# Two-layer graph attention on one core: the attention product of layer 1 computed graph by graph, with the high and low halves of h stacked over the rows

## The chip, the cores and the metric

The kernel runs on one core of a Trainium2 chip. Its engines work side by side and are tied by semaphores: TensorE (PE; its weight loads are shown apart, as PEld), VectorE (DVE), ScalarE (ACT), GpSimd (POOL), and SyncE (SP), which here only starts DMAs. The metric is the device time of one execution in microseconds (us). Less is better.

## The reference, cut to what matters

128 graphs of 64 nodes with 768 features pass through two layers, each with layer norm, relu, attention within the graph, and a residual. Layer 0 has 6 heads of 128 and the usual query, key, value and output projections. Layer 1 has 12 heads of 64:

```python
h = maximum(layernorm(x), 0)                     # 768 features of a node
hh = einsum('bnd,ade->bane', h, W)               # 12 heads of 64: "h" of the kernel
th = tanh(hh)
attn = th @ w_src + swapaxes(th @ w_dst, 2, 3)   # one number per pair of nodes and head
attn = softmax(where(adj, leaky(attn, 0.2), -999))
o = elu(einsum('banm,bame->bane', attn, hh) + b) # the product that is changed
gate = sigmoid(h @ H_w.T + H_b)
x = x + gate * o + (1 - gate) * h
```

## The kernel before, in words

Two graphs of 64 nodes fill the 128 partitions: that is a tile. Two tiles (t = 0, 1) make a group, and there are 32 groups. The program runs as a pipeline over groups. In step i the engines do layer 0 of group i, most of layer 1 of group j = i - 1, and the attention product and output of layer 1 of group p = i - 2. Steps 0, 1 and the last three are written out; the others are one loop body. Nothing is scheduled by a program: each engine has its own list of work, in the order in which `one(i, ...)` stands in its block, and waits on semaphores.

All large products use fp16 with a high and a low half for each operand. A product a*b is made of three fp16 matmuls, hi*hi + hi*lo + lo*hi, which add up in PSUM.

The order of PE in a step of the loop is: queries of i (two halves, L582), with the attention product of p for tile 0 behind them (`attend1`, L592 to L599); keys of i, with the attention product for tile 1 between their halves; values of i, tile 0; scores of layer 0 (L673, fp32); values, tile 1; the projection of j with W (`project_h`, tiles 0 and 1, L570); the gate's projection of tile 0; the context of layer 0 (L684); the operands of the logits of layer 1 (`logit_operands`, L702 and L706); the gate's projection of tile 1; the logits (L719); the output projection of layer 0. Each projection of one tile is 36 matmuls. `logit_operands` waits for `g_ready` of tile 0, since it writes into the PSUM bank that the gate's projection of tile 0 has filled and that DVE's `gate_argument` (L1100) reads.

What stands between the projection with W and that wait: ACT takes tanh (L1473) and the fp16 high half of h (L1477) out of PSUM. DVE takes the low half (`h_low`, L1082). POOL multiplies tanh by w_src and w_dst (`products`, L1690, L1691), and DVE sums over each head (L1072, L1077), splits the sums in three bf16 parts (L1110 to L1116) and then does `gate_argument` (L1100). POOL's products of tile 1 wait for `dst_ready` of tile 0, because both tiles use the same scratch. On DVE the order is: low part of h, source and target sums of tile 0; source sum, low part of h, target sum of tile 1; split; gate argument of tile 0.

The attention product of layer 1 works on a whole tile. The probabilities P of one head and tile are 128 x 64 (rows are the nodes of both graphs). They are written as fp16 high (ACT, `p1_high`, L1408) and low (DVE, `p1_low`, L926) halves into `e1`, where blocks of 64 columns alternate with zeroed gaps (POOL, L1737). SP's DMA transposes (L478) read graph 0 and graph 1 at offsets that differ by one block. So each head arrives in `pt1` as a 128 x 128 matrix with the two graphs on its diagonal and zeros elsewhere. It is the stationary operand of three matmuls of 64 columns per head; 12 heads make 36 matmuls per tile.

Of the kernel before, what the change touches and what calls it, by code (L numbers as in the profile page):

```python
# [25 lines left out]
F16 = mybir.dt.float16  # L26
# [3 lines left out]
ALU = mybir.AluOpType  # L30
# [51 lines left out]
def build_two_layer_gnn(nc, x, adj, wq, bq, wk, bk, wv, bv, wf, bf, wl, b1, w_src, w_dst, wg, bg, out):  # L82
# [13 lines left out]
    with ExitStack() as ctx:  # L96
# [72 lines left out]
        def split(first, shape, **k):  # L169

            v = units(first, 2).bitcast(F16)
            return [v[:, n * 2 * C:(n + 1) * 2 * C].rearrange(shape, **k) for n in range(2)]

        h1v_hi, h1v_lo = split(0, "p (t c) -> p t c", t=T)
        gate = tiles(2)
# [31 lines left out]
        e0 = spread(19 * C)  # L207
        e1 = spread(past_qt)

# [18 lines left out]
        spent = [w[:, WQ:WF + 1].rearrange("p m k n -> p (m k n)").bitcast(F32) for w in (w_hi, w_lo)]  # L228
        end_flat = w_lo[:, WQ].rearrange("p k n -> p (k n)")[:, 0:2 * SPREAD]
        end_e1 = [end_flat[:, n * SPREAD:(n + 1) * SPREAD] for n in range(2)]  # L230
        end_pt1 = halves(arena, 17 * C, a=H1)
# [204 lines left out]
        def _(sp):  # L436
# [32 lines left out]
            def transpose_rows(n, part, ht, g):  # L469
                after_held(sp, transposes_held, (hi_made, lo_made)[part][n], 2 * g + 2 if n else 2 * g)  # L470
                for t in range(T):
                    sp.dma_start_transpose(ht[:, :, t * P:(t + 1) * P], (h_hi, h_lo)[part][:, t, :])\  # L472
                        .then_inc(ht_landed[n], DMA)

            def transpose_blocks(pt, e, landed):
                for g in range(2):
                    r = slice(N * g, N * g + N)
                    sp.dma_start_transpose(pt[:, :, r], e[r, (1 - g) * N:(1 - g) * N + 2 * C]).then_inc(landed, DMA)  # L478

            def one(i, now, mid, last, nxt):  # L480
# [4 lines left out]
                def first_probabilities(g, zeroed):  # L485
                    after_held(sp, transposes_held, p1_gaps, zeroed)
                    after_held(sp, transposes_held, p1_hi_made, 2 * g + 1)
                    transpose_blocks(pt1[0][0], e1[0], pt1_hi_landed[0])
                    after_held(sp, transposes_held, p1_lo_made, 2 * g + 1)
                    transpose_blocks(pt1[0][1], e1[1], pt1_lo_landed[0])  # L490

                def second_probabilities():
                    sp.wait_ge(p1_hi_made, 2 * p + 2)
                    transpose_blocks(end_pt1[0], end_e1[0], pt1_hi_landed[1])
                    sp.wait_ge(p1_lo_made, 2 * p + 2)
                    transpose_blocks(end_pt1[1], end_e1[1], pt1_lo_landed[1])

# [16 lines left out]
                if last:  # L514
                    after_held(sp, transposes_held, p1_hi_made, 2 * p + 2)
                    after_held(sp, transposes_held, sum1_ready, 2 * p + 1)
                    transpose_blocks(pt1[1][0], e1[0], pt1_hi_landed[1])
                if mid:
# [5 lines left out]
                if last:  # L524
                    after_held(sp, transposes_held, p1_lo_made, 2 * p + 2)
                    after_held(sp, transposes_held, sum1_ready, 2 * p + 2)
                    transpose_blocks(pt1[1][1], e1[1], pt1_lo_landed[1])
                if mid:
# [32 lines left out]
        def _(pe):  # L561
# [30 lines left out]
            def attend1(t, g):  # L592
                for a in range(H1):
                    c = slice(a * E1, (a + 1) * E1)
                    pt1_hi, pt1_lo = pt1_of(t, g)
                    parts = ((pt1_hi, h1v_hi), (pt1_hi, h1v_lo), (pt1_lo, h1v_hi))
                    for n, (pt, hv) in enumerate(parts):
                        mm = nc.tensor.matmul(pair_att[t][:, c], pt[:, a, :], hv[:, t, c], start=(n == 0), stop=(n == 2))  # L598
                mm.then_inc(o_psum, 1)  # L599
# [25 lines left out]
            def one(i, now, mid, last, nxt):  # L625
# [30 lines left out]
                def attend(t):  # L656
                    if t == 0:
                        pe.wait_ge(h_ready, 2 * p + 2)
# [147 lines left out]
        def _(dve):  # L806
# [121 lines left out]

# [86 lines left out]
            def one(i, now, mid, last, nxt):  # L1015
                j, p = i - 1, i - 2
                first = isinstance(i, int) and i == 0
                tail, final = mid and not now, last and not mid
                def h_low(t):
                    dve.wait_ge(th_ready, 2 * j + t + 1)  # L1020
# [59 lines left out]
                def h_low(t):  # L1080
                    dve.wait_ge(h_hi_ready, 2 * j + t + 1)
                    nc.vector.scalar_tensor_tensor(h1v_lo[:, t, :], pair_prj[t][:, 0:C], HV, h1v_hi[:, t, :],  # L1082
                                                   ALU.mult, ALU.subtract).then_inc(h_ready, 1)

# [290 lines left out]
        def _(act):  # L1375
# [22 lines left out]
            def p1_high(t, g):  # L1398
# [57 lines left out]
            def one(i, now, mid, last, nxt):  # L1456
# [8 lines left out]
                def h_parts(t):  # L1465
# [145 lines left out]
        def _(pool):  # L1611
# [36 lines left out]
            def one(i, now, mid, last, nxt):  # L1648
# [82 lines left out]
                if mid:  # L1731
                    keep_copy()
                    products(0)
                    products(1)
                    target_terms()
                    after_held(pool, gaps_held, ct_psum, 2 * i + 2)
                    nc.gpsimd.memset(gaps(past_qt), 0.0).then_inc(p1_gaps, 1)  # L1737
                    if not nxt:
                        nc.gpsimd.memset(gaps_in(end_flat), 0.0).then_inc(end_gaps, 1)
                if now:  # L1740
# [38 lines left out]
```

## Time and profile before

| | |
|---|---|
| time, median of 3 runs | 2560.9 us (2559.81 to 2561.69) |
| time of the profiled execution | 2561.74 us |
| its span | 2559.9 us |
| PE busy | 2498.9 us, 98% of the span |
| DVE busy | 2003.8 us, 78% |
| ACT, POOL busy | 908.3 us (35%), 804.6 us (31%) |
| one step of the loop | 77.2 us |
| granted TensorE clock, mean | 0.99 of full speed |

The profiled execution lies 1.84 us above its own span, and within 1 us of the median. The page lists busy time by engine and by group of instructions. The timeline view lists instructions with their start, and so shows who is late at a given place. In it, lengths of matmuls include their way through the array; the rate of a row of matmuls is read from starts. PE's row of instructions in one step repeats every 77.2 us almost to the hundredth, so one step stands for all of them.

### The profile page before, as it was taken

How to read it: one execution, taken by the hardware profiler on the slowest of the kernel's cores; microseconds unless marked ns; L12 is line 12 of the kernel's file. 1: busy time of each engine (PE TensorE's matmuls, PEld its weight loads, DVE VectorE, ACT ScalarE, POOL GpSimd, SP SyncE). 2: the span in 40 equal slices, each digit the busy share in tenths (PEclk: the TensorE clock that was granted, in tenths of full speed). 3: DMA queues.
4: the chain of work that ended last, by engine and by line, in shares of the span. 5: the costliest groups of instructions: out<-in, count | busy, mean ns of one | idle time of the engine just before them, and what ended most of it. 6: DMA issues, size and time to landing. Idle time of an engine off the chain costs nothing.

```text
span 2559.9 us, 51824 instructions
## 1 busy us (share of the span) xinstructions
PE 2498.9 (98%) x21440; PEld 1789.9 (70%) x21440; DVE 2003.8 (78%) x2704; ACT 908.3 (35%) x1054; POOL 804.6 (31%) x564
## 2 busy tenths in 40 slices
PE   7999999999999999999999999999999999999995
PEld 5766777776777776777766777766777766777763
DVE  7768777778787788777787787787787787787778
ACT  5333333233333333333333333333333343332332
POOL 1133332333332333322333323333323333323334
PEclk9999999999999999999999999999999999999997
DMA  8243343443343443443433443433433433434432
GB/s 297 44 76 80 80 99 74 80 81 76 83 96 73 84 80 74 86 92 69 92 75 75 90 87 74 91 72 77 93 83 75 89 73 76 97 79 75 81 58 54
DMA packets 552301, 216.94 MB, mean 85 GB/s; under 512 B 517840, under 2 KB 527056, under 8 KB 552272
## 3 DMA queue, kind: packets, MB, share of 16 engines
q1 hardware_dynamic: 552272, 216.53, 40.6%
q8 instruction: 21, 0.34, 0.1%
q14 instruction: 8, 0.07, 0.0%
HBM read 67.02 MB, written 25.17 MB: 36 GB/s over the span
## 4 chain that ended last, share of the span: by engine, by line
PE 94%; DVE 3%; ACT 1%; DMA 1%; POOL 0%; SPq 0%; issue 0%; DVEq 0%
PE pair_prj L570 56%; PE pair_prj L582 29%; PE pair_att L684 3%; PE pair_att L598 3%; PE pair_att L673 2%; PE pair_att L719 1%; DMA arena<-in_L_gnn_Wq 0%; DVE w_lo L865 0%; PE pair_prj L706 0%; PE pair_prj L608 0%; SPq L472 0%; DVE w_top L825 0%; SPq L478 0%; POOL arena L1660 0%; DVE w_hi L954 0%
## 5 line engine op out<-in xcount | busy, mean ns | idle before, releaser
L570 PE MATMUL pair_prj<-w_hi,arena 128*128 128x512 f16 (+1 forms) x6144 | 1443.7, 327 | 6.4 <-DVE arena L1082 6.1
L570 PE MATMUL pair_prj<-w_lo,arena 128*128 128x512 f16 (+1 forms) x3072 | 1003.2, 327 | 0.0
L570 PEld LDWEIGHTS pair_prj<-w_hi,arena 128*128 128x128 f16 x6144 | 601.8, 98 | 416.0 <-issue 10.4
L582 PE MATMUL pair_prj<-arena,w_hi 128*128 128x256 f16 x4608 | 762.3, 273 | 3.5 <-DVE w_lo L872 3.3
L582 PE MATMUL pair_prj<-arena,w_lo 128*128 128x256 f16 x2304 | 629.3, 273 | 0.0
L582 PEld LDWEIGHTS pair_prj<-arena,w_hi 128*128 128x128 f16 x4608 | 447.4, 98 | 55.6 <-issue 3.4
L570 PEld LDWEIGHTS pair_prj<-w_lo,arena 128*128 128x128 f16 x3072 | 301.2, 98 | 199.5 <-issue 2.5
L1638 POOL TENSOR_TENSOR rstd<-var_eps,minus_half 128x2 f32<-128x2 f32 x63 | 62.8, 997 | 695.4 <-DVE var_eps L890 688.5
L582 PEld LDWEIGHTS pair_prj<-arena,w_lo 128*128 128x128 f16 x2304 | 225.9, 98 | 26.6
L1655 POOL TENSOR_TENSOR arena<-arena,b_row 128x768 f32<-128x768 f32 x60 | 108.6, 1809 | 331.0 <-DVE arena L947 331.0
L1388 ACT ACTIVATE h_hi<-arena,shift,rstd 128x768 f16<-128x768 f32 x124 | 120.6, 1020 | 215.0 <-DVE shift L895 215.0
L1690 POOL TENSOR_TENSOR arena<-arena,src_row 128x768 f32<-128x768 f32 x62 | 113.6, 1832 | 246.0 <-ACT arena L1473 246.0
L1660 POOL TENSOR_TENSOR arena<-arena 128x768 f32<-128x768 f32 x60 | 126.5, 2108 | 152.5 <-ACT arena L1419 152.5
L907 DVE TENSOR_TENSOR arena<-arena,h_hi 128x768 f16<-128x768 f32 x124 | 161.4, 1342 | 3.6 <-ACT arena L1388 3.6
L1424 ACT ACTIVATE arena<-arena 128x768 f32<-128x768 f32 x60 | 50.7, 845 | 283.1 <-DVE arena L954 283.1
L911 DVE SCALAR_TENSOR_TENSOR arena<-pair_prj,w_undo,bk_col 128x768 f32<-128x768 f32 x64 | 65.1, 1018 | 109.6 <-PE pair_prj L582 109.6
L1691 POOL TENSOR_TENSOR arena<-arena,dst_row 128x768 f32<-128x768 f32 x62 | 132.8, 2142 | 0.0
L1419 ACT ACTIVATE arena<-arena,keep_shift,keep_rstd 128x768 f32<-128x768 f32 x60 | 61.2, 1020 | 192.0 <-DVE arena L975 192.0
L1388 ACT ACTIVATE arena<-arena,shift,rstd 128x768 f32<-128x768 f32 x128 | 123.7, 1013 | 11.6 <-DVE shift L895 6.2
L877 DVE BATCH_NORM_STATS2 bn_out<-arena 128x6 f32<-128x384 f32 x252 | 121.7, 545 | 2.3 <-DMA arena<-in_x 2.3
L1745 POOL TENSOR_TENSOR arena<-arena,bf_row 128x768 f32<-128x768 f32 x64 | 115.6, 1828 | 6.1 <-DVE bf_row L1149 6.1
L1487 ACT ACTIVATE arena<-arena 128x768 f32<-128x768 f32 x62 | 52.4, 844 | 183.1 <-DVE arena L1100 183.1
(180 smaller groups left out, 2905.6 us busy)
## 6 DMA issues: line engine op xcount, KB each, us to landing
arena<-in_x SPq DMA_DIRECT2D x64, 768.0 KB, 4.3
out<-arena SPq DMA_DIRECT2D x64, 384.0 KB, 2.3
arena<-arena SPq DMA_TRANSPOSE x380, 3.4
arena<-in_L_gnn_Wq SPq DMA_DIRECT2D x2, 1152.0 KB, 8.5
arena<-in_L_gnn_Wk SPq DMA_DIRECT2D x2, 1152.0 KB, 11.8
w_hi<-in_L_gnn_Wv SPq DMA_DIRECT2D x2, 1152.0 KB, 13.5
w_lo<-in_L_gnn_Wf SPq DMA_DIRECT2D x2, 1152.0 KB, 14.4
arena<-in_L_gnn_W SPq DMA_DIRECT2D x2, 1152.0 KB, 13.2
```

Source lines behind the costliest of these rows:

```text
L570: mm = nc.tensor.matmul(pair[:, lo:hi], lhs(a, k), weight(m, k, b)[:, lo:hi], start=(k == 0 and n == 0), stop=(k == KT - 1 and n == 2))
L582: mm = nc.tensor.matmul(pair[:, c * 256:(c + 1) * 256], weight(m, k, a)[:, o:o + P], (ht0_hi, ht0_lo)[b][:, k, :], start=(k == 0 and n == ...
L598: mm = nc.tensor.matmul(pair_att[t][:, c], pt[:, a, :], hv[:, t, c], start=(n == 0), stop=(n == 2))
L684: mm = nc.tensor.matmul(pair_att[t][:, h * P:(h + 1) * P], v[:, t, h * P:(h + 1) * P], pt[:, t * H0 + h, :], start=(n == 0), stop=(n == 2))
L877: bn = nc.vector.bn_stats(bn_out[n][:, t, c, :], src[:, t, c * (C // 2):(c + 1) * (C // 2)])
L907: nc.vector.tensor_tensor(h_lo[:, t, :], rows[:, t, :], h_hi[:, t, :], ALU.subtract)\
L1388: return nc.scalar.activation(dst[:, t, :], src[:, t, :], ACT.Relu, bias=shift[n][:, t:t + 1], scale=rstd[n][:, t:t + 1])
L1655: nc.gpsimd.tensor_tensor(o, o, b1_row[:].unsqueeze(1).broadcast_to([P, H1, E1]), ALU.add)\
L1660: nc.gpsimd.tensor_tensor(held(g)[:, t, :], held(g)[:, t, :], scratch(t, g)[2], ALU.add)\
L1690: nc.gpsimd.tensor_tensor(by_src, th, src_row[:], ALU.mult).then_inc(src_prod, 1)
L1691: nc.gpsimd.tensor_tensor(by_dst, th, dst_row[:], ALU.mult).then_inc(dst_prod, 1)
L1745: nc.gpsimd.tensor_tensor(x1[:, t, :], x1[:, t, :], bf_row[:], ALU.add).then_inc(bf_added, 1)
```

## The change

The product P*h of layer 1 is computed for each graph of a tile apart. For graph b, the high half of h (64 nodes) is placed on partitions 0 to 63 and the low half on partitions 64 to 127 of one operand, `h1v[b]`. The probabilities are transposed so that P_hi of a head stands on both halves of the partitions. One matmul over 128 rows then gives P_hi*h_hi + P_hi*h_lo. A second one, with P_lo above and zeros below, adds P_lo*h_hi. The stationary operand is 64 columns wide, and graph b writes PSUM partitions 64b to 64b + 63.

- PE: per head 2 x 2 matmuls with a 64-column stationary operand, in place of 3 with 128 columns; 48 per tile in place of 36.
- ACT: `p1_high` writes each block of 64 twice (1536 elements per partition in place of 768). The high half of h is taken graph by graph, in two instructions over 64 partitions.
- DVE: `h_low` becomes two instructions over 64 partitions. One reads PSUM and the high half and writes 64 partitions further up. `p1_low` keeps its size.
- POOL: only the gaps of the low halves are zeroed, 768 elements in place of 1664.
- SP: the transposes of probabilities read 128 partitions x 768 each, in place of 64 x 1536; their number stays. The counts of `h_ready` and `h_hi_ready` double.

```diff
-        h1v_hi, h1v_lo = split(0, "p (t c) -> p t c", t=T)
+        h1v = split(0, "p (t c) -> p t c", t=T)
...
+            def transpose_heads(pt, e, landed):
+                for n in range(2):
+                    a = slice(n * H0, (n + 1) * H0)
+                    sp.dma_start_transpose(pt[:, a, :], e[:, a].rearrange("p a z n -> p (a z n)")).then_inc(landed, DMA)
...
-                    parts = ((pt1_hi, h1v_hi), (pt1_hi, h1v_lo), (pt1_lo, h1v_hi))
-                    for n, (pt, hv) in enumerate(parts):
-                        mm = nc.tensor.matmul(pair_att[t][:, c], pt[:, a, :], hv[:, t, c], start=(n == 0), stop=(n == 2))
+                    for n, pt in enumerate((pt1_hi, pt1_lo)):
+                        for b in range(2):
+                            r = slice(b * N, (b + 1) * N)
+                            mm = nc.tensor.matmul(pair_att[t][r, c], pt[:, a, r], h1v[b][:, t, c],
+                                                  start=(n == 0), stop=(n == 1))
...
-                    pe.wait_ge(h_ready, 2 * j + t + 1)
+                    pe.wait_ge(h_ready, 4 * j + 2 * t + 2)
...
-                nc.vector.scalar_tensor_tensor(blocks(e_lo), p1[:, t], P_TOP, blocks(e_hi), ALU.mult, ALU.subtract)\
-                    .then_inc(p1_lo_made, 1)
+                nc.vector.scalar_tensor_tensor(e_lo[:, :, 0, :], p1[:, t], P_TOP, e_hi[:, :, 0, :], ALU.mult,
+                                               ALU.subtract).then_inc(p1_lo_made, 1)
...
-                    dve.wait_ge(h_hi_ready, 2 * j + t + 1)
-                    nc.vector.scalar_tensor_tensor(h1v_lo[:, t, :], pair_prj[t][:, 0:C], HV, h1v_hi[:, t, :],
-                                                   ALU.mult, ALU.subtract).then_inc(h_ready, 1)
+                    for b in range(2):
+                        dve.wait_ge(h_hi_ready, 4 * j + 2 * t + b + 1)
+                        nc.vector.scalar_tensor_tensor(h1v[b][N:P, t, :], pair_prj[t][b * N:(b + 1) * N, 0:C], HV,
+                                                       h1v[b][0:N, t, :], ALU.mult, ALU.subtract).then_inc(h_ready, 1)
...
-                nc.scalar.activation(blocks(e1_of(t, g)[0]), p1[:, t], ACT.Copy, scale=P_TOP).then_inc(p1_hi_made, 1)
+                nc.scalar.activation(e1_of(t, g)[0], p1[:, t].unsqueeze(2).broadcast_to([P, H1, 2, N]), ACT.Copy,
+                                     scale=P_TOP).then_inc(p1_hi_made, 1)
...
-                    nc.scalar.activation(h1v_hi[:, t, :], pair_prj[t][:, 0:C], ACT.Copy, scale=HV)\
-                        .then_inc(h_hi_ready, 1)
+                    for b in range(2):
+                        nc.scalar.activation(h1v[b][0:N, t, :], pair_prj[t][b * N:(b + 1) * N, 0:C], ACT.Copy, scale=HV)\
+                            .then_inc(h_hi_ready, 1)
...
-                    nc.gpsimd.memset(gaps(past_qt), 0.0).then_inc(p1_gaps, 1)
+                    nc.gpsimd.memset(e1[1][:, :, 1, :], 0.0).then_inc(p1_gaps, 1)
```

PE in the loop, from the last query matmul to the first key matmul, tile 0 (L582 is the projection, L598 the attention product), before:

```order
L582 MATMUL pair_prj1<-arena,w_hi 128x256 x2
L582 MATMUL pair_prj1<-arena,w_lo 128x256
L598 MATMUL pair_att0<-arena 128x64 [waits pt1_lo_landed0,pt1_hi_landed0,h_ready]
L598 MATMUL pair_att0<-arena 128x64 x35
L582 MATMUL pair_prj0<-arena,w_hi 128x256 [waits q_ready]
```

And in the changed kernel (L588 and L605 are the same two lines):

```order
L588 MATMUL pair_prj1<-arena,w_hi 128x256 x2
L588 MATMUL pair_prj1<-arena,w_lo 128x256
L605 MATMUL pair_att0<-arena 64x64 [waits pt1_lo_landed0,pt1_hi_landed0,h_ready]
L605 MATMUL pair_att0<-arena 64x64 x47
L588 MATMUL pair_prj0<-arena,w_hi 128x256 [waits q_ready]
```

The 36 matmuls have become 48, with moving operand and neighbours in the same order; only their shape and number differ.

DVE in the loop, from the low parts of the next group's layer 0 to the split of the sums (L1082 is `h_low`, L1072 and L1077 the source and target sums), before:

```order
L1082 SCALAR_TENSOR_TENSOR arena<-pair_prj0,arena 128x768 [waits h_hi_ready]
L1072 TENSOR_REDUCE src_dst<-arena 128x12 [waits src_prod]
L1077 TENSOR_REDUCE src_dst<-arena 128x12 [waits dst_prod]
L1072 TENSOR_REDUCE src_dst<-arena 128x12 [waits src_prod]
L1082 SCALAR_TENSOR_TENSOR arena<-pair_prj1,arena 128x768 [waits h_hi_ready]
L1077 TENSOR_REDUCE src_dst<-arena 128x12 [waits dst_prod]
L1110 CAST parts<-src_dst 128x4x12 [waits dst_ready,src_ready]
```

And in the changed kernel (L1086 is `h_low`, L1075 and L1080 the sums; ISA and REGISTER_ALU compute the values of waits):

```order
L1086 SCALAR_TENSOR_TENSOR arena<-pair_prj0,arena 64x768 [waits h_hi_ready]
L1085 REGISTER_ALU
L1086 SCALAR_TENSOR_TENSOR arena<-pair_prj0,arena 64x768 [waits h_hi_ready]
L1075 TENSOR_REDUCE src_dst<-arena 128x12 [waits src_prod]
L1080 TENSOR_REDUCE src_dst<-arena 128x12 [waits dst_prod]
L1075 TENSOR_REDUCE src_dst<-arena 128x12 [waits src_prod]
L1085 REGISTER_ALU
L1086 SCALAR_TENSOR_TENSOR arena<-pair_prj1,arena 64x768 [waits h_hi_ready]
L1085 REGISTER_ALU
L1086 SCALAR_TENSOR_TENSOR arena<-pair_prj1,arena 64x768 [waits h_hi_ready]
L1080 TENSOR_REDUCE src_dst<-arena 128x12 [waits dst_prod]
L1114 CAST parts<-src_dst 128x4x12 [waits dst_ready,src_ready]
```

Each `h_low` has become two instructions; the second pair stands between the source and the target sum of tile 1.

## Rows read from the trace of the kernel before

**Rows 1.** Page, busy time, share of the span and instructions.
```profile
PE 2498.9 (98%) x21440; PEld 1789.9 (70%) x21440; DVE 2003.8 (78%) x2704; ACT 908.3 (35%) x1054; POOL 804.6 (31%) x564
```

**Rows 2.** Windows view of one steady group: span, then busy time (count) by engine.
```profile
1002.10:1079.30 77.20, 77.20 (x671) 55.46 (x669) 60.77 (x82) 27.11 (x33) 24.95 (x17) 1.00 0.41 82
```

**Rows 3.** Timeline, weight loads, in the steady group and in the tail: start, length, what.
```profile
1079.25 0.18 PEld L702 LDWEIGHTS pair_prj<-node_eye,dst_terms 128*108 128x108 bf16 x2
...
2519.71 0.17 PEld L702 LDWEIGHTS pair_prj<-node_eye,dst_terms 128*108 128x108 bf16 x2 [3.85 <-POOL dst_terms L1697]
```

**Rows 4.** Timeline, DVE, from the first low part of h.
```profile
1069.37 0.94 DVE L1082 SCALAR_TENSOR_TENSOR arena<-pair_prj,arena 128x768 f16<-128x768 f32 x1
1070.24 0.94 DVE L1072 TENSOR_REDUCE src_dst<-arena 128x12 f32<-128x768 f32 x1
1071.15 0.95 DVE L1077 TENSOR_REDUCE src_dst<-arena 128x12 f32<-128x768 f32 x1
1074.46 0.95 DVE L1072 TENSOR_REDUCE src_dst<-arena 128x12 f32<-128x768 f32 x1 [2.36 <-POOL arena L1690]
1075.33 0.95 DVE L1082 SCALAR_TENSOR_TENSOR arena<-pair_prj,arena 128x768 f16<-128x768 f32 x1
1076.22 0.95 DVE L1077 TENSOR_REDUCE src_dst<-arena 128x12 f32<-128x768 f32 x1
...
1078.10 1.01 DVE L1100 SCALAR_TENSOR_TENSOR arena<-pair_prj,w_undo,bg_row 128x768 f32<-128x768 f32 x1
```

**Rows 5.** Timeline, POOL then ACT, the same stretch.
```profile
1072.62 1.81 POOL L1690 TENSOR_TENSOR arena<-arena,src_row 128x768 f32<-128x768 f32 x1 [1.50 <-ACT arena L1473]
...
1071.64 0.90 ACT L1473 ACTIVATE arena<-pair_prj,w_undo 128x768 f32<-128x768 f32 x1 [4.25 <-PE pair_prj L570]
1072.44 0.80 ACT L1477 ACTIVATE arena<-pair_prj 128x768 f16<-128x768 f32 x1
```

**Rows 6.** Timeline, DVE and weight load, first graph group.
```profile
151.09 1.02 DVE L1100 SCALAR_TENSOR_TENSOR arena<-pair_prj,w_undo,bg_row 128x768 f32<-128x768 f32 x1
...
152.85 0.18 PEld L702 LDWEIGHTS pair_prj<-node_eye,dst_terms 128*108 128x108 bf16 x2
```

**Rows 7.** Timeline, PE, one attention of layer 1 and its neighbours.
```profile
1032.50 1.21 PE L598 MATMUL pair_att<-arena 128*128 128x64 f16 x36
1033.55 0.27 PE L582 MATMUL pair_prj<-arena,w_hi 128*128 128x256 f16 x1
```

**Rows 8.** Timeline, PE, the scores of layer 0 and their neighbours.
```profile
1052.13 0.27 PE L570 MATMUL pair_prj<-w_hi,arena 128*128 128x256 f16 x1
1052.33 1.62 PE L673 MATMUL pair_att<-arena 128*64 128x64 f32 x48
1053.88 0.39 PE L570 MATMUL pair_prj<-w_hi,arena 128*128 128x512 f16 x1
```

**Rows 9.** Groups of instructions: busy us, mean ns, idle before.
```profile
L702 PEld LDWEIGHTS pair_prj<-node_eye,dst_terms 128*108 128x108 bf16 x64 | 5.9, 128 | 3.8 <-POOL dst_terms L1697 3.8
...
L706 PEld LDWEIGHTS pair_prj<-ident_bf,parts 128*36 128x36 bf16 x64 | 3.7, 96 | 1.3
...
L1123 DVE TENSOR_TENSOR arena<-pair_prj,of_head 108x768 bf16<-108x768 f32 x64 | 60.5, 947 | 0.4 <-PE pair_prj L702 0.4
...
L1408 ACT ACTIVATE arena<-p_place 128x768 f16<-128x768 f32 x62 | 52.3, 843 | 54.0 <-DMA arena<-arena 51.1
...
L1562 ACT ACTIVATE arena<-zero 128x1664 f16<-128x1664 f32 x32 | 50.4, 1574 | 1.5 <-PE pair_att L673 1.5
```

**Rows 10.** Timeline, PE, end of the second projection with W.
```profile
1071.33 0.49 PE L570 MATMUL pair_prj<-w_hi,arena 128*128 128x256 f16 x2
```

**Rows 11.** Chain of waits in the tail: start, length, what.
```profile
2509.12 0.95 DVE arena L1082
...
2518.67 0.94 DVE w_lo L1100
...
2533.26 0.85 ACT w_lo L1408
```

More of the change, by code:

```diff
@@ L207, in build_two_layer_gnn @@
         e0 = spread(19 * C)
-        e1 = spread(past_qt)
+        e1 = [arena[:, past_qt + n * C:past_qt + (n + 1) * C].bitcast(F16).rearrange("p (a z n) -> p a z n", z=2, n=N)
+              for n in range(2)]
         def blocks(e):
@@ L228, in build_two_layer_gnn @@
         spent = [w[:, WQ:WF + 1].rearrange("p m k n -> p (m k n)").bitcast(F32) for w in (w_hi, w_lo)]
-        end_flat = w_lo[:, WQ].rearrange("p k n -> p (k n)")[:, 0:2 * SPREAD]
-        end_e1 = [end_flat[:, n * SPREAD:(n + 1) * SPREAD] for n in range(2)]
+        end_flat = w_lo[:, WQ].rearrange("p k n -> p (k n)")
+        end_e1 = [end_flat[:, 2 * n * C:2 * (n + 1) * C].rearrange("p (a z n) -> p a z n", z=2, n=N) for n in range(2)]
         end_pt1 = halves(arena, 17 * C, a=H1)
@@ L487, in first_probabilities @@
                     after_held(sp, transposes_held, p1_hi_made, 2 * g + 1)
-                    transpose_blocks(pt1[0][0], e1[0], pt1_hi_landed[0])
+                    transpose_heads(pt1[0][0], e1[0], pt1_hi_landed[0])
                     after_held(sp, transposes_held, p1_lo_made, 2 * g + 1)
-                    transpose_blocks(pt1[0][1], e1[1], pt1_lo_landed[0])
+                    transpose_heads(pt1[0][1], e1[1], pt1_lo_landed[0])
                 def second_probabilities():
                     sp.wait_ge(p1_hi_made, 2 * p + 2)
-                    transpose_blocks(end_pt1[0], end_e1[0], pt1_hi_landed[1])
+                    transpose_heads(end_pt1[0], end_e1[0], pt1_hi_landed[1])
                     sp.wait_ge(p1_lo_made, 2 * p + 2)
-                    transpose_blocks(end_pt1[1], end_e1[1], pt1_lo_landed[1])
+                    transpose_heads(end_pt1[1], end_e1[1], pt1_lo_landed[1])
                 def store(g, t):
@@ L516, in one @@
                     after_held(sp, transposes_held, sum1_ready, 2 * p + 1)
-                    transpose_blocks(pt1[1][0], e1[0], pt1_hi_landed[1])
+                    transpose_heads(pt1[1][0], e1[0], pt1_hi_landed[1])
                 if mid:
@@ L526, in one @@
                     after_held(sp, transposes_held, sum1_ready, 2 * p + 2)
-                    transpose_blocks(pt1[1][1], e1[1], pt1_lo_landed[1])
+                    transpose_heads(pt1[1][1], e1[1], pt1_lo_landed[1])
                 if mid:
@@ L657, in attend @@
                     if t == 0:
-                        pe.wait_ge(h_ready, 2 * p + 2)
+                        pe.wait_ge(h_ready, 4 * p + 4)
                     pe.wait_ge(pt1_hi_landed[t], GRAPHS * (p + 1))
@@ L1018, in one @@
                 tail, final = mid and not now, last and not mid
-                def h_low(t):
-                    dve.wait_ge(th_ready, 2 * j + t + 1)
-                    nc.vector.scalar_tensor_tensor(h1v_lo[:, t, :], pair_prj[t][:, 0:C], HV, h1v_hi[:, t, :],
-                                                   ALU.mult, ALU.subtract).then_inc(h_ready, 1)
                 def source_and_target(t):
@@ L1080, in h_low @@
                 def h_low(t):
-                    dve.wait_ge(h_hi_ready, 2 * j + t + 1)
-                    nc.vector.scalar_tensor_tensor(h1v_lo[:, t, :], pair_prj[t][:, 0:C], HV, h1v_hi[:, t, :],
-                                                   ALU.mult, ALU.subtract).then_inc(h_ready, 1)
+                    for b in range(2):
+                        dve.wait_ge(h_hi_ready, 4 * j + 2 * t + b + 1)
+                        nc.vector.scalar_tensor_tensor(h1v[b][N:P, t, :], pair_prj[t][b * N:(b + 1) * N, 0:C], HV,
+                                                       h1v[b][0:N, t, :], ALU.mult, ALU.subtract).then_inc(h_ready, 1)
                 def context_low(t):
@@ L1736, in one @@
                     after_held(pool, gaps_held, ct_psum, 2 * i + 2)
-                    nc.gpsimd.memset(gaps(past_qt), 0.0).then_inc(p1_gaps, 1)
+                    nc.gpsimd.memset(e1[1][:, :, 1, :], 0.0).then_inc(p1_gaps, 1)
                     if not nxt:
-                        nc.gpsimd.memset(gaps_in(end_flat), 0.0).then_inc(end_gaps, 1)
+                        nc.gpsimd.memset(end_e1[1][:, :, 1, :], 0.0).then_inc(end_gaps, 1)
                 if now:
```

## The prediction

> **What bounds the kernel now.** I read the page first. PE is busy for 98% of the span, DVE for 78% [rows 1]. So what PE executes, and where it waits, is the time. The windows view of one step of the loop says it more sharply: PE is busy for all of the 77.20 us, DVE for 60.77, ACT for 27.11 [rows 2]. No wait shows. But a wait that is just met does not show either, so I looked at each place at which PE depends on another engine, and at how long before PE's arrival the other engine is done.
>
> One place has no room. PE takes the first weight load of `logit_operands` (L702) at 1079.25, without idle time [rows 3]. It waits there for DVE's `gate_argument` of tile 0 (L1100), which starts at 1078.10 and ends at 1079.11 [rows 4]. The signal needs time too: in the tail PE does wait at L702 and loads at 2519.71 [rows 3], and L1100 there ends at 2519.61 [rows 11], so 0.10. Of the 0.14 us only 0.04 is free. DVE has the following list before L1100: low part of h, source sum, target sum of tile 0, then source sum, low part, target sum of tile 1 [rows 4]. The changed kernel lengthens this very list.
>
> **PE's own work.** Before, an attention product of one tile takes 1.05 us from its first matmul to the next projection's first (1032.50 to 1033.55) for 36 matmuls: 0.029 each [rows 7]. After, it is 48 matmuls with 64-column weights, in 24 pairs whose members use different column halves and different weights. The only row of such a shape are the scores of layer 0, in fp32: 48 matmuls from 1052.33, whose group lasts 1.62 with a last matmul of about 0.22, so 24 pairs in 1.40, 0.058 a pair [rows 8]. Around them PE loses time: they start at 1052.33 where the matmul before them, 0.11 long in a stream, would let them start at 1052.24; and the next projection starts at 1053.88, 0.15 behind 1053.73. That is 0.24 per block, with the 0.09 ahead.
>
> Below: the 24 pairs at the 0.029 of one fp16 matmul and no loss around them, 0.70 us, 0.35 less than now. Above: 0.058 as in fp32 and the loss, 1.39 + 0.24 = 1.63, 0.58 more. I take 0.030 a pair, since the moving operand is the same 64 fp16 columns as in [rows 7] and only fp32 doubles the price, and the whole loss of 0.24, since the change of array shape is the same: 0.72 + 0.24 = 0.96, 0.09 less. There are 64 such products: -5.8 us. Ends: -22 and +37.
>
> The length of a weight load could speak against the 0.030. Here the loads show 128 ns for 108 columns and 96 ns for 36 [rows 9], which is 0.44 ns per column, so 28 ns for 64, still under 0.030, and both halves of the array load at once in [rows 8]. The Trainium skill, TensorE: Matmul & The Clock Gate, section LDWEIGHTS, gives a load as its columns divided by 1.2 in ns, and TensorEngine Tiling (Array Packing), Restrictions, says that column tiling switches off the fast weight load. By these two a 64-column load would take 53 ns, an estimate. The slope in this trace disagrees with that figure, by which 108 and 36 columns would lie 60 ns apart and not 32; no fp16 load of 64 columns stands in the trace.
>
> **The list on DVE.** `h_low` becomes two instructions over 64 partitions and the same 768 elements. The multiply over 108 partitions (L1123) takes 947 ns [rows 9], what those over 128 take, so I count no discount for fewer partitions: each `h_low` adds one start-to-start distance, 1069.37 to 1070.24, 0.87 us [rows 4].
>
> Tile 0: the low part ends 0.87 later, at 1071.18. PE's gate projection waits for it; PE's last matmul before that starts at 1071.33 + 0.11 and the load just ahead of it, at about 1071.33 [rows 10]. With 0.10 for the signal that is met by 0.05. Should it miss, PE waits there and DVE catches up by as much, so it costs nothing more. The target sum of tile 0 ends at 1072.10 + 0.87 = 1072.97. POOL's products of tile 1 wait for it. They start at 1072.62 now, 0.08 after the tanh of tile 1 ends at 1072.54 [rows 5]. After, they start 0.08 after 1072.97, at 1073.05: 0.43 later. The idle time of 2.36 us ahead of DVE's next sum [rows 4] looks like room, but it is this wait for POOL, so it moves along instead of absorbing.
>
> Tile 1: source sum 0.43 later; then one more `h_low`, 0.87; the target sum would wait for POOL's second product, which ends 0.43 later than now and is early. So the target sum, the split and L1100 come 1.30 later, and L702 1.30 - 0.04 = 1.26 us later. All of PE's step stands behind it, and what DVE does after it is itself released by PE, so each step gets longer by it. In the first group L1100 ends at 152.11 and PE comes at 152.85 [rows 6], so 0.64 is free and 0.66 remains. 30 x 1.26 + 0.66 = +38.5 us. The loop now computes the waits' values between the halves; below, that is free; above, one gap of 0.11 for each of three, 0.33 x 31 = +10. I take nothing, since DVE is busy while they are prepared. A price below nothing for the list is excluded, as nothing is removed from it.
>
> **The rest.** `p1_high` goes from 768 to 1536 elements. 843 ns for 768 and 1574 for 1664 [rows 9] give 0.82 ns per element, so 0.63 us more, 1.47 in all. ACT has 50 us of idle time in a step [rows 2], and both pieces are read by DMAs and DVE several us before PE asks, so nothing in the loop. The second instruction for the high half of h, 0.80 us [rows 5], ends at 1074.04, before DVE's low part of tile 1 at 1075.76. POOL's memset gets shorter and was in nobody's way. The transposes keep their bytes and number. All this counts nothing, which is the end from below; from above, if the cover of `p1_high` failed, it is 0.63 in each of 31 steps, +20.
>
> In the tail the chain of waits itself runs through DVE and ACT: `h_low` (L1082), `gate_argument` (L1100) and `p1_high` (L1408) stand in it [rows 11]. Two of `h_low` and two of `p1_high` get longer there, at most by 2 x 0.87 + 2 x 0.63 = 3.0, and I take it whole, since little idle time stands between them; the end below is 0.
>
> **Sum.** 38.5 - 5.8 + 3.0 = +35.7 us. The span of 2559.9 becomes 2595.6; the execution lies 1.84 above its span, 2597.4; the median of the runs is 0.84 below the profiled execution, so 2596.6. I forecast 2597 us, 1.4% slower.
>
> **Rivals.**
> A. The loads of 64 columns hold PE up, so that a pair costs what the fp32 pair does, 0.058. The attention products then cost +37 in place of -5.8: 2640. For it: the fp32 pair fits either reading, a slow load or a slow pass. Against: the slope of [rows 9]. Chance 0.15. With the 53 ns of the Trainium skill's page named above, a product would take 24 x 0.053 + 0.24 = 1.51, and the time would be 2632, an estimate.
> B. The pairs cost 0.029 and the shape changes without loss: 2597 - 17 = 2580. For it: the loss in [rows 8] may belong to fp32. Against: nothing else changes there. Chance 0.10.
> C. The other side: instructions over 64 partitions take half as long, because a half of them is idle. Then the two halves of `h_low` together cost what one does, L1100 is not late, L702 waits for nothing, and PE keeps the gain of its attention products: 2561 - 5.8 + 1.3 for `p1_high` in the tail = 2556, or 2540 with B's pairs. It decides from where the delay of L1100 is under 0.09 x 2 + 0.04 = 0.22 us. For it: nothing but the absence of a row over 64 partitions. Against: 108 partitions have no discount at all. Chance 0.06.
> D. The delay is there but half of it is taken up, by DVE instructions being ahead elsewhere: +19 less, 2578. For it: DVE has 16 us idle in a step. Against: every idle time before L1100 is a wait for POOL or PE. Chance 0.05.
>
> **Chances and range.** The forecast itself has 0.64, within 2593 to 2615 (from no cost in the tail to 10 us for the waits' values and 24 x 0.005 x 64 = 8 for slower pairs). What a measurement can tell from no change is 0.2%, 5 us. Slower by more: forecast, A, B and D, 0.64 + 0.15 + 0.10 + 0.05 = 0.94, less 0.03 for what I haven't seen: 0.91. C is split between faster and same by its pairs, and what I haven't seen goes there too: faster 0.05, same 0.04. The range takes in the forecast, B, D and the lower part of A, between the 0.035 and the 0.055 of a pair, and leaves out C and A's upper end: 2577 to 2633.
>
> **What would show it.** PE's waits must list L702's line for DVE's gate argument 30 times at about 1.3 us. The step must be 77.20 + 1.26 - 0.18 = 78.3 us. DVE's `h_low` must show 128 instructions of about 0.95 us. The attention products must take about 0.96 us from first matmul to the next projection's. The forecast is wrong if the half-size instructions are shorter, if PE does not wait there, or if a pair takes 0.05 us or more.

## The result, and the profile after

The changed kernel takes 2636.89 us, the median of 4 runs (2636.17 to 2639.15), against 2561.3 us before (4 runs, 2559.81 to 2561.74): a ratio of 1.0299, 95% interval 1.0287 to 1.0312. It is 3.0% slower. The forecast was 2597 us with a range of 2577 to 2633: the direction is right, the loss is twice the one forecast, and the time lies above the range. The profiled execution of the changed kernel is the longest of its four (2639.15 us), so what is counted in its trace sums to 77.4 us, where the medians lie 75.6 apart.

Page of the kernel after, as in [rows 1], with one group:

```profile
PE 2520.1 (96%) x22208; PEld 1774.6 (67%) x22208; DVE 2075.4 (79%) x2768; ACT 1003.8 (38%) x1118; POOL 775.5 (29%) x564
...
L1086 DVE SCALAR_TENSOR_TENSOR arena<-pair_prj,arena 64x768 f16<-64x768 f32 x128 | 122.4, 956 | 7.5 <-ACT arena L1483 3.6
```

PE's share fell and DVE's rose by one point, so PE waits for something. `h_low` (L1086 now) is there 128 times at 956 ns, the same as over 128 partitions. Lines are 3 to 8 higher than before: `h_low` L1082 is L1086, the source and target sums L1072 and L1077 are L1075 and L1080, `gate_argument` L1100 is L1104, the logit operands L702 are L710, the attention product L598 is L605, POOL's products L1690 and L1691 are L1696 and L1697, `p1_high` L1408 is L1412.

The waits view of the kernel after: who waits for whom, us in total, how often, the longest. Before, PE waits for DVE at this line nowhere in the loop.

```profile
PE pair_prj L710 <- DVE arena L1104: 51.8, 30, 1.8
...
POOL arena L1696 <- DVE src_dst L1080: 66.5, 29, 2.3
```

This is the place and the number of times that were forecast, with 1.75 us instead of 1.3 in 29 of them and 1.10 in the last. The windows view of two steps in a row, from one logit operand to the next (columns as in [rows 2]), shows that this isn't all:

```profile
1030.40:1111.16 80.76, 79.02 (x693) 55.23 (x693) 63.01 (x84) 30.11 (x35) 24.09 (x18) 0.98 0.36 78
1111.16:1190.24 79.08, 77.33 (x693) 54.81 (x693) 63.00 (x84) 30.11 (x35) 24.11 (x18) 1.00 0.37 80
```

There are two kinds of step. 19 take 79.07 us, the last one 78.38, and 10 take about 80.77, at a granted clock of 0.98 of the full one; before, all 30 take 77.20. The same view around the wait at the start of the first of these steps:

```profile
1028.60:1030.40 1.80, 0.06 (x2) 0.00 (x0) 1.62 (x4) 0.02 (x1) 1.02 (x2) 1.00 0.00 0
1030.40:1032.00 1.60, 1.60 (x10) 0.87 (x11) 0.00 (x0) 1.58 (x3) 1.60 (x2) 1.00 0.00 0
1032.00:1035.40 3.40, 3.40 (x10) 1.19 (x9) 3.31 (x4) 1.01 (x3) 2.01 (x2) 0.50 0.00 0
```

PE is idle up to 1030.40 and works from then on, and at 1032.0 the granted clock falls to 0.50, which is the lower level, 1.2 GHz, for 3.4 us. The work of these 3.4 us takes 1.70 longer (80.77 - 79.07). The loop has 10 such dips between 233 and 2305 us; before it had none between 147.7 and 2492.7.

DVE's list in a steady step, timeline of the kernel after, against [rows 4], and POOL's and PE's rows against [rows 5] and [rows 7]:

```profile
1096.78 2.57 DVE L915 TENSOR_TENSOR arena<-arena,h_hi 128x768 f16<-128x768 f32 x1
1099.38 1.95 DVE L1086 SCALAR_TENSOR_TENSOR arena<-pair_prj,arena 64x768 f16<-64x768 f32 x2
1101.36 0.95 DVE L1075 TENSOR_REDUCE src_dst<-arena 128x12 f32<-128x768 f32 x1
1102.23 0.94 DVE L1080 TENSOR_REDUCE src_dst<-arena 128x12 f32<-128x768 f32 x1
1105.15 0.95 DVE L1075 TENSOR_REDUCE src_dst<-arena 128x12 f32<-128x768 f32 x1 [1.98 <-POOL arena L1696]
1106.13 1.94 DVE L1086 SCALAR_TENSOR_TENSOR arena<-pair_prj,arena 64x768 f16<-64x768 f32 x2
1108.10 0.95 DVE L1080 TENSOR_REDUCE src_dst<-arena 128x12 f32<-128x768 f32 x1
...
1109.85 0.21 DVE L1120 TENSOR_TENSOR parts<-rest,parts 128x48 bf16<-128x48 f32 x1
1110.08 1.02 DVE L1104 SCALAR_TENSOR_TENSOR arena<-pair_prj,w_undo,bg_row 128x768 f32<-128x768 f32 x1
```

```profile
1103.31 1.80 POOL L1696 TENSOR_TENSOR arena<-arena,src_row 128x768 f32<-128x768 f32 x1 [2.30 <-DVE src_dst L1080]
```

```profile
1062.42 0.27 PE L588 MATMUL pair_prj<-arena,w_lo 128*128 128x256 f16 x1
1062.62 0.95 PE L605 MATMUL pair_att<-arena 128*64 128x64 f16 x48
1063.50 0.39 PE L588 MATMUL pair_prj<-arena,w_hi 128*128 128x256 f16 x2
```

Read DVE's rows by their starts. Two sums over 128 partitions stand 0.87 apart, each starting 0.08 before its predecessor's end (1101.36, 1102.23). An `h_low` starts 0.03 after its predecessor's end, and so does what follows it: 1099.35 to 1099.38, 1101.33 to 1101.36, 1106.10 to 1106.13. Two cost 1.98, and the overlap is lost at both borders. Even L1104, behind L1120, has it no more (1110.06 to 1110.08; before it overlapped by 0.08), although both are over 128 partitions. So the number of partitions can't be what decides; the last section says what the borders have in common.

**Where the 77.4 us went** (span 2637.3 against 2559.9). The first group's logit operands come 1.0 later; 29 steps are 1.87 longer and the last one 1.18, 55.4; the 10 dips cost 16.9; from the last step's logit operands to the end it takes 95.06 instead of 91.01, 4.05. Sum 77.4.

### The profile page after: what moved, and what is told of

It is laid out like the page before. It is cut to its first block, busy times and chain, and to the rows that moved or that the text cites. A ratio compares the mean times of both kernels' runs of the same rounds, so it can differ in the third digit from the quotient of the medians.

```text
span 2637.3 us, 53662 instructions
## 1 busy us (share of the span) xinstructions
PE 2520.1 (96%) x22208; PEld 1774.6 (67%) x22208; DVE 2075.4 (79%) x2768; ACT 1003.8 (38%) x1118; POOL 775.5 (29%) x564
## 4 chain that ended last, share of the span: by engine, by line
PE 55%; DVE 26%; ACT 8%; issue 7%; POOL 3%; DMA 1%; SPq 0%; DVEq 0%; ACTq 0%; POOLq 0%
PE pair_prj L588 29%; PE pair_prj L576 23%; DVE arena L1086 4%; DVE arena L980 3%; DVE bn_out L885 2%; ACT arena L1392 2%; DVE src_dst L1080 2%; POOL arena L1696 2%; PE pair_att L605 2%; ACT arena L1568 2%; DVE arena L915 2%; ACT h_hi L1392 1%; DVE src_dst L1075 1%; DVE arena L1104 1%; DVE p_place L1065 1%
## 5 line engine op out<-in xcount | busy, mean ns | idle before, releaser
L576 PE MATMUL pair_prj<-w_hi,arena 128*128 128x512 f16 (+1 forms) x6144 | 1458.4, 329 | 8.0 <-DVE arena L1086 7.6
L588 PE MATMUL pair_prj<-arena,w_hi 128*128 128x256 f16 x4608 | 763.0, 273 | 3.5 <-DVE w_lo L880 3.3
L588 PE MATMUL pair_prj<-arena,w_lo 128*128 128x256 f16 x2304 | 629.3, 273 | 0.0
L588 PEld LDWEIGHTS pair_prj<-arena,w_hi 128*128 128x128 f16 x4608 | 446.8, 98 | 58.0 <-issue 3.4
L588 PEld LDWEIGHTS pair_prj<-arena,w_lo 128*128 128x128 f16 x2304 | 225.9, 98 | 26.5
L1696 POOL TENSOR_TENSOR arena<-arena,src_row 128x768 f32<-128x768 f32 x62 | 113.5, 1830 | 269.1 <-ACT arena L1478 202.6
L1697 POOL TENSOR_TENSOR arena<-arena,dst_row 128x768 f32<-128x768 f32 x62 | 132.7, 2141 | 0.0
L1086 DVE SCALAR_TENSOR_TENSOR arena<-pair_prj,arena 64x768 f16<-64x768 f32 x128 | 122.4, 956 | 7.5 <-ACT arena L1483 3.6
```

What stands on the lines that cost most here:

```text
L576: mm = nc.tensor.matmul(pair[:, lo:hi], lhs(a, k), weight(m, k, b)[:, lo:hi], start=(k == 0 and n == 0), stop=(k == KT - 1 and n == 2))
L588: mm = nc.tensor.matmul(pair[:, c * 256:(c + 1) * 256], weight(m, k, a)[:, o:o + P], (ht0_hi, ht0_lo)[b][:, k, :], start=(k == 0 and n == ...
L1086: nc.vector.scalar_tensor_tensor(h1v[b][N:P, t, :], pair_prj[t][b * N:(b + 1) * N, 0:C], HV, h1v[b][0:N, t, :], ALU.mult, ALU.subtract).th ...
L1696: nc.gpsimd.tensor_tensor(by_src, th, src_row[:], ALU.mult).then_inc(src_prod, 1)
L1697: nc.gpsimd.tensor_tensor(by_dst, th, dst_row[:], ALU.mult).then_inc(dst_prod, 1)
```

## The experiments

The ratios of experiments 1 to 4 are to 13 runs of the kernel before with a median of 2560.74 us, those of 5 to 8 to 13 runs with 2561.16. The theory after the result: DVE's list, dearer than forecast, and the clock as a consequence of PE's wait. Its rivals: the array's side costs more than forecast (rival A), or the dips belong to the new matmuls. The counts of dips are those of one profiled execution each. Line numbers differ by a few from kernel to kernel.

**1. The array's side alone.** The kernel before, with attention products of 48 matmuls of 64 columns and no change of `h_low`. It leaves out P_hi*h_lo, so it is a probe and no kernel to use.

```
-                    parts = ((pt1_hi, h1v_hi), (pt1_hi, h1v_lo), (pt1_lo, h1v_hi))
-                    for n, (pt, hv) in enumerate(parts):
-                        mm = nc.tensor.matmul(pair_att[t][:, c], pt[:, a, :], hv[:, t, c], start=(n == 0), stop=(n == 2))
+                    for n, (pt, hv) in enumerate(((pt1_hi, h1v_hi), (pt1_lo, h1v_hi))):
+                        for b in range(2):
+                            r = slice(b * N, (b + 1) * N)
+                            mm = nc.tensor.matmul(pair_att[t][r, c], pt[:, a, r], hv[:, t, c],
+                                                  start=(n == 0), stop=(n == 1))
```

> The kernel before with only the matmuls of the attention product in the new shape: 48 of 64 columns per tile in place of 36 of 128, over the operands of before (so the low half of h takes no part in the product). Theory 1 (the array's side is a small gain and the loss lies elsewhere): each product goes from 1.05 us to about 0.98 with the two changes of array shape around it, as in the trace of the changed kernel; 64 x -0.066 = -4.2 us, so 2557. Rival (the change of array shape costs more when PE does not wait elsewhere in the step, or weights hold it up): 2561 or above.

2556.63 us, ratio 0.9984 (0.9975 to 0.9994): 4.1 us faster. All steps take 77.07, 0.13 less than before, PE waits nowhere in the loop, and the clock is full in it. Rival A is false, and the new matmuls don't bring the dips.

**2. DVE's side alone.** The kernel before, with `h_low` in two instructions over 64 partitions, each on its own partitions.

```
-                    nc.vector.scalar_tensor_tensor(h1v_lo[:, t, :], pair_prj[t][:, 0:C], HV, h1v_hi[:, t, :],
-                                                   ALU.mult, ALU.subtract).then_inc(h_ready, 1)
+                    for b in range(2):
+                        r = slice(b * N, (b + 1) * N)
+                        low = nc.vector.scalar_tensor_tensor(h1v_lo[r, t, :], pair_prj[t][r, 0:C], HV, h1v_hi[r, t, :],
+                                                             ALU.mult, ALU.subtract)
+                    low.then_inc(h_ready, 1)
```

> The kernel before with only DVE's low part of h split into two instructions over 64 partitions, each reading and writing its own partitions; nothing moves across partitions and no wait is added. Theory 1 (an instruction over 64 partitions does not overlap with its neighbours on DVE: 0.98 to 0.99 us start to start, where two over 128 take 0.87): L1100 comes about 2.0 late, PE waits 1.75 to 1.8 us at the operands of the logits, the clock dips as in the changed kernel, 2636 to 2642. Rival (the lost overlap belongs to the move from one half of the partitions to the other, or to the waits computed in between): 0.87 start to start, PE waits 1.3 us, 2600 to 2615.

2639.92 us, ratio 1.0308 (1.029 to 1.0325). This one edit brings the whole loss. PE's wait is 1.75 us again, the steps take 79.12 and 80.82, and 11 dips stand in the loop. By the medians it is 3.0 above the changed kernel, by the spans of the two profiled executions 1.8. In these, one dip more costs 1.7 and the steps without dips another 1.8 (0.05 each: the array gives nothing back here, but the first half of tile 0 keeps its overlap); the first logit operands come 0.9 earlier, and the tail is 0.8 shorter. DVE's timeline, the pair of tile 0 and its predecessor, then tile 1, and the waits view:

```profile
1096.66 2.57 DVE L907 TENSOR_TENSOR arena<-arena,h_hi 128x768 f16<-128x768 f32 x1
1099.15 1.91 DVE L1084 SCALAR_TENSOR_TENSOR arena<-pair_prj,arena 64x768 f16<-64x768 f32 x2
...
1104.89 0.95 DVE L1072 TENSOR_REDUCE src_dst<-arena 128x12 f32<-128x768 f32 x1 [1.98 <-POOL arena L1693]
1105.88 1.92 DVE L1084 SCALAR_TENSOR_TENSOR arena<-pair_prj,arena 64x768 f16<-64x768 f32 x2
1107.83 0.95 DVE L1077 TENSOR_REDUCE src_dst<-arena 128x12 f32<-128x768 f32 x1
```

```profile
PE pair_prj L702 <- DVE arena L1103: 51.9, 30, 1.8
```

In tile 0 the pair starts at 1099.15, 0.08 before L907 ends at 1099.23, as a 128-partition instruction does. In tile 1, 1104.89 to 1107.83 is 2.94, for a pair that took 1.76 before (1074.46 to 1076.22 in [rows 4]): 1.18 more, not 0.87. The waits ahead of the sums are those of before, so the values that a loop computes for its waits don't make these gaps.

**3. and 4. The same list, longer by instructions over 128 partitions.** One extra sum of 768 elements ahead of each `h_low`; in the fourth, ahead of tile 1's alone.

```
                     dve.wait_ge(h_hi_ready, 2 * j + t + 1)
+                    after(dve, spare_done, 2 * j + t)
+                    nc.vector.tensor_reduce(spare[:], heads1(pair_prj[t][:, 0:C]), AX_X, ALU.add).then_inc(spare_done, 1)
```

> The kernel before with one more DVE instruction over all 128 partitions in front of each low part of h (sums over heads out of the same PSUM, written to a place nobody reads). Theory 1: it overlaps with its neighbours, 0.87 start to start, so L1100 is late by 0.43 + 0.87 and PE waits 1.26 us a step, +39 us: 2602 if the clock stays at full speed, and some 15 us more if waits of this length bring the same dips to half clock as those of 1.75 us. Rival (any added instruction costs what the changed kernel's cost, 1.1 us each): PE waits 1.8 us, 2636 or more.

> As before, with that one more instruction only for tile 1. Theory 1: L1100 is late by 0.87, PE waits 0.83 us a step, +26 us: 2587, with the clock at full speed; if the clock dips with waits of this length too, each dip adds 1.7 us, up to 17: 2604. Rival (the idle time of 2.36 us on DVE takes up part of it): under 2580.

2598.44 us, ratio 1.0147 (1.013 to 1.0164), and 2585.77, 1.0098 (1.0082 to 1.0115). The steps take 78.42 and 77.99, 1.22 and 0.79 more than before, the waits are 1.04 and 0.61, and neither has a dip in the loop. So the forecast's term was the right price, 1.26 a step, for an added instruction over 128 partitions, its share through POOL included (1.22 less 0.79 is 0.43). Timeline of the third kernel, tile 1, with the extra sum in the second row:

```profile
1087.22 0.95 DVE L1074 TENSOR_REDUCE src_dst<-arena 128x12 f32<-128x768 f32 x1 [1.99 <-POOL arena L1694]
1088.09 0.95 DVE L1085 TENSOR_REDUCE spare<-pair_prj 128x12 f32<-128x768 f32 x1
1088.95 0.95 DVE L1086 SCALAR_TENSOR_TENSOR arena<-pair_prj,arena 128x768 f16<-128x768 f32 x1
1089.81 0.94 DVE L1079 TENSOR_REDUCE src_dst<-arena 128x12 f32<-128x768 f32 x1
```

0.86 to 0.87 from start to start throughout. The second kernel has one instruction more per tile too, and is 41.5 us slower. The spans of the two profiled executions lie 42.7 apart: 1.2 up to the first logit operands, 20.8 in the 30 steps (0.70 each, 0.48 in the last), 18.8 for the 11 dips, 1.9 in the tail.

**5. Is it the wait's length or the 64 partitions that makes the dips?** The third kernel with a second extra sum for tile 1: 128 partitions everywhere, and a wait as long as the changed kernel's.

```
+                    for n in range(1 + t):
+                        after(dve, spare_done, 3 * j + t)
+                        nc.vector.tensor_reduce(spare[:, n], heads1(pair_prj[t][:, 0:C]), AX_X, ALU.add)\
+                            .then_inc(spare_done, 1)
```

> The kernel before with more full instructions over all 128 partitions in front of the low part of h: one for tile 0, two for tile 1 (sums nobody reads); no instruction over 64 partitions, no change of array shape beyond that of before. PE's wait becomes 1.04 + 0.87 = 1.9 us a step, step 79.3. Theory 1 (dips to half clock follow from PE's wait of this length, whatever makes it): a dip of 3.4 us in about every third step, +17 us: 2640 (2632 to 2648). Rival (dips belong to the new instructions): no dips, 2624.

2647.52 us, ratio 1.0335 (1.0318 to 1.0353), 7.5 above the expected 2640 and just inside its bounds. Waits and windows of it:

```profile
PE pair_prj L704 <- DVE arena L1106: 56.9, 31, 1.9
```

```profile
1033.60:1037.00 3.40, 3.40 (x10) 1.17 (x9) 3.05 (x4) 1.27 (x3) 3.27 (x2) 0.50 0.00 0
```

With a wait of 1.90 us, 14 of 30 steps have a dip of 3.4 us (80.97 instead of 79.28). The profiled execution is the longest of four, 2649.74 us; the shortest takes 2645.49, so by 1.70 a dip it would have 11 or 12, an estimate. The dips follow PE's wait, whatever makes it.

**6. Low part of tile 1 into the idle time.** The changed kernel, with `h_low(1)` ahead of the source sum of tile 1, where DVE waits for POOL anyway.

```
                     h_target(0)
-                    h_source(1)
                     h_low(1)
+                    h_source(1)
                     h_target(1)
```

> The changed kernel, with one step of DVE's list moved: both halves of the low part of h of tile 1 ahead of the source sum of tile 1, into the idle time in which DVE waits for POOL there. Theory 1 (the loss is the list on DVE before gate_argument, and the clock's dips follow from the wait that it makes): what stays is POOL's late start, 0.79 us; PE waits about 0.8 us a step, no dips after 148 us; step 77.9 us, 2583 (2578 to 2592). Rival (the array's new shape or the doubled p1_high carries part of the loss, or the dips come from the shape): 2600 or more.

2584.9 us, ratio 1.0094 (1.0077 to 1.0111), 52 less than the changed kernel. The wait is 0.57, the step 77.89, no dip in the loop: 30 x 1.18 = 35 for the steps and 17 for the dips.

**7. POOL's wait.** The changed kernel, with the source product of tile 1 waiting for the source sum of tile 0 and only the target product for the target sum.

```
-                        pool.wait_ge(dst_ready, 2 * j + 1)
+                        pool.wait_ge(src_ready, 2 * j + 1)
                     nc.gpsimd.tensor_tensor(by_src, th, src_row[:], ALU.mult).then_inc(src_prod, 1)
+                    if t == 1 and not tail:
+                        pool.wait_ge(dst_ready, 2 * j + 1)
```

> The changed kernel, with POOL's source product of tile 1 waiting for the source sum of tile 0 only, and the target product for the target sum, in place of both for the latter. Theory 1: POOL starts at tanh's end again, 0.79 us earlier; L1104 stays 1.3 us late; PE waits about 1.2 us a step; step 78.3, 2602 if the clock does not dip (as it did not with waits of 1.04 us), up to 17 more if it does. Rival (POOL's start does not matter, DVE's list alone does): as the changed kernel, 2637.

2597.29 us, ratio 1.0141 (1.0124 to 1.0158). The wait is 0.96 (expected 1.2), the step 78.29, 0.78 shorter than 79.07, and the loop has no dip. The step is as expected; the 2602 expected from it lies 5 too high. This is the share of the delay that ran through POOL, and with it gone the dips are gone too.

**8. Both moves.**

> Both of these edits together. Theory 1: L1104 is late by at most 0.2 us, PE's wait at the operands of the logits is under 0.2 us a step, the shorter attention products give 0.13 back; step 77.1 to 77.3, 2559 to 2567 with some 3 us more in the tail. Rival (loss beside the list on DVE): 2575 or more.

2562.7 us (10 runs), ratio 1.0007 (0.9997 to 1.0017): as fast as before. A step in the windows view:

```profile
1076.57:1153.69 77.12, 77.12 (x696) 54.76 (x694) 63.02 (x85) 30.10 (x34) 24.14 (x17) 1.00 0.37 82
```

PE never waits for L1104 in the loop, and its step is 0.08 shorter than before, 2.3 in all. The tail, 95.04 us against 91.01, takes this away. The first logit operands come 1.7 earlier in this execution, a point that lies between 150.6 and 153.9 us in the ten traces, so that the spans are equal is in part chance. In the tail the chain of waits still runs through two pairs of `h_low` and two longer `p1_high`:

```profile
2512.50 0.95 DVE arena L1086
2513.45 0.03 issue
2513.48 0.96 DVE arena L1086
2514.44 0.03 issue
2514.48 0.95 DVE src_dst L1075
...
2527.42 1.49 ACT arena L1412
```

None of these kernels with the whole computation beats the kernel before. A tail with another order was not tried.

## Why the forecast was right in direction and wrong in size

| Term | Forecast | Measured in the changed kernel |
|---|---|---|
| DVE's list, first group | +0.66 | +1.0, at another place |
| DVE's list, 30 steps | +37.8 | +59.3 (+55.4 for the steps, +3.9 that the array gave back) |
| Attention products | -5.8 | -3.9 in the loop |
| Clock dips in the loop | not in the sum | +16.9 |
| Tail | +3.0 | +4.05 |
| Sum | +35.7 | +77.4 on the span |

**What bounds the kernel, and where it would break.** Right. The place with no room was L702 behind L1100, and PE now waits there 30 times. In the loop the gate projection, too, is just met or missed by 0.05, as said. For the first group this was read wrong. There PE already waits at the gate projection for `h_low`, before and after:

```profile
142.48 0.58 PE L570 MATMUL pair_prj<-w_hi,arena 128*128 128x512 f16 x1 [4.09 <-DVE arena L1082]
```

```profile
144.00 0.59 PE L576 MATMUL pair_prj<-w_hi,arena 128*128 128x512 f16 x1 [5.33 <-DVE arena L1086]
```

Of the 1.52 us between these two, 0.98 is the second half of `h_low`, and 0.54 has passed before it starts (141.91 against 141.37). About 0.5 comes back since fewer of the matmuls behind it run at the lower clock, which lasts until 147.7 and 147.9. L710 then follows L1104 without a wait worth the name (ends at 153.77, loads at 153.88). So +1.0 is near +0.66 by luck.

**The failed step: the distance in DVE's list.** The forecast said that "each `h_low` adds one start-to-start distance, 1069.37 to 1070.24, 0.87 us". The duration was right (956 ns, no discount for 64 partitions; rival C is false). But the 0.87 holds an overlap with the neighbour, and this was taken over from rows whose instructions all start at the same partition to instructions that don't, of which no row existed. Measured against the tanh of tile 1 on ACT (1071.64 before, 1101.54 after), the pieces are:
- the first `h_low` starts 0.11 later and the target sum of tile 0 ends 1.17 later, forecast 0.87;
- POOL's first product starts 0.79 later, forecast 0.43: the 0.44 of room is used once, so each further 0.1 in the list passes whole, and 0.06 more goes at the handover (0.14 instead of 0.08);
- the `h_low` of tile 1 adds 1.19 (source sum to target sum 2.95 instead of 1.76), forecast 0.87;
- behind the split, 0.11 more from the lost overlap at L1104.

So L1104 starts 0.79 + 1.19 + 0.11 = 2.09 later, forecast 1.30. Experiments 3 and 4 show that the method was right and the input wrong: the same sum with 128-partition instructions gave 1.26, and 1.22 was measured. The upper bound set for the list (+10 for the waits' values) was half of what came, 21.5 with the 30 steps alone, and was put on another cause.

**The missing term: the clock.** No term of the forecast stood for what a wait on PE does to PE's clock afterwards. In the kernel before PE never waits in the loop, so its trace there shows no such case; but in its tail the granted clock falls to the lower level three times, and that could have raised the question. The first fall, at 2492.7 us, comes 0.9 after PE has waited 3.27 us for DVE at L598, the second, at 2520.0, 0.3 after the wait of 3.85 us at L702 [rows 3] (windows view, columns as in [rows 2]):

```profile
2492.70:2496.10 3.40, 3.40 (x23) 2.24 (x20) 1.96 (x4) 1.67 (x3) 0.00 (x0) 0.50 1.10 113
2520.00:2526.80 6.80, 5.96 (x16) 1.95 (x17) 6.63 (x8) 2.36 (x4) 2.78 (x3) 0.50 0.01 2
```

Experiments 2 to 8 show that the dips go with the wait: 14 at 1.90 us, 10 and 11 at 1.75, none at 1.04 or less. What lies between 1.04 and 1.75 wasn't measured. The forecast's own wait of 1.26 lies in that gap, so whether it would have brought dips is open; but the second error stands on the first, which made the wait as long as it is.

**The array's side.** Right, but for a gain of 4.1 us where 5.8 were forecast. An attention product takes 0.88 from its first matmul to the next projection's, with 0.09 ahead of it: 0.97, forecast 0.96, before 1.05. Its 24 pairs stand 0.032 apart (forecast 0.030), the change of shape costs 0.09 ahead and 0.11 behind (0.88 less 24 x 0.032), forecast 0.24 in all, so rival B is false as well. Experiment 1 measures this side alone, -4.1. Two weight loads of 64 columns and their matmuls come every 32 ns; a load is recorded with 113 to 116 ns from start to end, so loads overlap. The Trainium skill, TensorE: Matmul & The Clock Gate, section LDWEIGHTS, would give it 53 ns, an estimate; the trace does not agree.

**The tail.** It was sized with the same 0.87: `p1_high` is as forecast (1.49 for 1.47), and the two `h_low` cost more. Experiment 2, which changes only these, has a tail of 94.24, 3.2 longer than before, where 2 x 0.87 = 1.74 were forecast. The granted clock is at the lower level for 45 us of this tail, for 41 of experiment 2's and for 37 of the one before; what this costs wasn't told apart from the rest.

**The range.** It was kept to 2633, since rival A's upper end was cut off. The two causes that came were in none of the rivals.

## What to carry to other kernels

A start-to-start distance between instructions holds for rows like these alone, of the same form and from the same first partition: for what the trace doesn't show, count the full duration and a gap at both borders as the upper bound. An engine that never waits has nothing in its trace on what a wait costs it: where a change makes TensorE wait in each step, put the clock into the sum as a term with bounds, and look for the granted clock wherever the trace does show a wait. And when a list in front of a just-met deadline has to grow, look for an idle time inside the list and for a wait that asks for more than it needs; here two such moves gave back the whole loss.

## What was not expected of the hardware

- DVE instructions over 64 partitions take as long as those over 128: for 768 elements, the 128 halves of `h_low` take 956 ns (950 to 962), where the 64 whole ones took 948 (943 to 958).
- Whether two DVE neighbours overlap went with the partition at which they start, not with how many they span. Between `h_low` and L1104, where nothing else was waited for, an instruction started 0.08 us before its predecessor's end if it read PSUM and SBUF from the same first partition as the last instruction that had read there, and wrote to the same as the last that had written. If one of these differed, it started 0.01 to 0.03 after that end, so a border cost up to 0.11 more. In the changed kernel the first half of `h_low` writes from partition 64 behind writes from 0, the second reads PSUM from 64, and the next sum writes from 0 again: the overlap is lost at each of these borders. In experiment 2 the first half of tile 0 spans 64 partitions but starts where its predecessors did, and it overlaps by 0.08; the first half of tile 1 reads PSUM from 0 after a half that read it from 64, and starts 0.03 late. L1104 (L1103 in experiment 2) spans 128 partitions and reads PSUM from 0, also behind a half that read it from 64: it has lost its overlap in every kernel with split `h_low` and kept 0.08 in every other. The 25 loop steps looked at in each of the ten traces fit this. No run was made to test it, and why the engine does so is open.
- PE waits of 1.75 us once in a step of 79 us brought the lower clock level for 3.4 us in about every third step, 0.3 to 1.6 us after PE had started again, and waits of 1.90 us in about every second. Each such dip costs 1.70 us of PE's work.
- fp16 matmuls of 64 columns in alternating column halves, each with its own weights, run at 0.032 us a pair, little over half of the 0.058 that fp32 takes for the same shape [rows 8].
